# Indirect gathers of a graph convolution, issued without their bounds check

## The reference

```
deg  = segment_sum(1, dst);  norm = deg[src]**-0.5 * deg[dst]**-0.5
for (W, b) in three layers:
    h = segment_sum((h @ W)[src] * norm, dst) + b
out = layernorm(x + h)
```

## Time and profile before

| | us |
|---|---|
| three executions, median | 3550.75 (3549.87 to 3553.59) |
| span of the profiled execution | 3868.5 |
| GpSimd busy in it | 2587.0 (67%) |
| TensorE busy in it | 2756.2 (71%) |
| VectorE busy | 1462.3 (38%) |
| ScalarE busy | 383.0 (10%) |

### The profile page before, as it was taken

The page is one execution under the profiler, slowest core; times in us unless marked ns, Lnnn a source line. Parts: engine busy times, 40 slices in busy tenths (PEclk is TensorE's granted clock), DMA queues, the critical chain, the costliest instruction groups (busy, mean ns, idle before and its releaser), DMA issues.

```text
span 3868.5 us, 33824 instructions
## 1 busy us (share of the span) xinstructions
PE 2756.2 (71%) x6732; PEld 1145.6 (30%) x6782; DVE 1462.3 (38%) x3181; ACT 383.0 (10%) x581; POOL 2587.0 (67%) x2511
## 2 busy tenths in 40 slices
PE   7677777777777767677766667675666677676675
PEld 5233333333333322222222222222222222222222
DVE  6344444544444422222222222222333333333334
ACT  1122222222222200000000000000000000000000
POOL 0677676776766747776766767666676677676765
PEclk8888888988888889988899999988998988989988
DMA  8566666666666646666666666665676666666765
GB/s 299 172 186 185 176 188 181 189 180 175 184 184 179 187 128 191 191 190 183 192 187 188 194 190 197 184 192 172 193 206 196 199 201 203 193 202 196 206 195 167
DMA packets 243709, 735.25 MB, mean 190 GB/s; under 512 B 43286, under 2 KB 44946, under 8 KB 243664
## 3 DMA queue, kind: packets, MB, share of 16 engines
q0 software_dynamic: 199440, 653.68, 59.2%
q1 hardware_dynamic: 44224, 81.08, 5.8%
HBM read 683.39 MB, written 51.20 MB: 190 GB/s over the span
## 4 chain that ended last, share of the span: by engine, by line
issue 22%; another core or an unknown queue 13%; PE 9%; POOL 7%; DMA 6%; DVE 4%; DVEq 2%; POOLq 1%; SPq 0%; ACT 0%; ACTq 0%
PE ps L587 9%; POOL ring L427 7%; DMA ring<-y_dram,idx_stage 5%; DVE acc L966 1%; DVEq L963 1%; DVE onehot L923 1%; DVE idx_stage L914 1%; POOLq L427 0%; DMA y_dram<-acc 0%; DVE h_sb L988 0%; DVEq L966 0%; DVE ln L994 0%; DMA out_dram<-row_sb 0%; DVE h_sb L974 0%
## 5 line engine op out<-in xcount | busy, mean ns | idle before, releaser
L427 POOL DMA_INDIRECT ring<-y_dram,idx_stage x2493 | 2584.1, 1037 | 1258.0 <-issue 761.4
L587 PE MATMUL ps<-ring,onehot 128*128 128x512 f32 x4570 | 2293.4, 650 | 833.7 <-DMA ring<-y_dram,idx_stage 586.8
L587 PEld LDWEIGHTS ps<-ring,onehot 128*128 128x128 f32 x4570 | 910.3, 207 | 2148.4 <-issue 1800.6
L914 DVE COPY idx_stage<-src_idx 128x4 int32 (+1 forms) x624 | 111.9, 180 | 1836.4 <-remote 767.8
L966 DVE SCALAR_TENSOR_TENSOR acc<-ps,mask,acc 128x512 f32 x624 | 440.1, 745 | 91.3 <-issue 74.0
L923 DVE TENSOR_TENSOR onehot<-place_iota,lo_f 128x512 f32<-128x512 f32 (+1 forms) x624 | 400.9, 643 | 1.1 <-issue 0.6
L611 PE MATMUL ps<-w,w_sb 128*128 128x512 f32 x376 | 225.9, 757 | 127.5 <-issue 89.6
L717 ACT ACTIVATE acc<-h_sb,dinv 128x512 f32 (+1 forms) x96 | 69.3, 722 | 1399.3 <-DVE h_sb L974 901.8
L611 PEld LDWEIGHTS ps<-w,w_sb 128*128 128x128 f32 x376 | 91.0, 249 | 243.8 <-issue 199.8
L721 ACT ACTIVATE ln<-ln 128x1 f32<-128x1 f32 x49 | 9.9, 203 | 1231.2 <-DVE ln L1000 586.3
L594 PE MATMUL ps<-wT,w_sb 128*128 128x512 bf16 x234 | 82.3, 409 | 54.1 <-DVE wT L945 51.3
(11 more groups left out here) (121 smaller groups left out, 783.8 us busy)
## 6 DMA issues: line engine op xcount, KB each, us to landing
ring<-y_dram,idx_stage POOLq DMA_INDIRECT x2493
y_dram<-acc SPq DMA_DIRECT2D x96, 256.0 KB
acc<-in_x_dram SPq DMA_DIRECT2D x1, 12288.0 KB
y_dram<-acc SPq DMA_DIRECT2D x12, 1024.0 KB
w_sb<-in_x_dram SPq DMA_DIRECT2D x48, 256.0 KB
out_dram<-row_sb SPq DMA_DIRECT2D x48, 256.0 KB
w_sb<-in_L_gnn_W_dram SPq DMA_DIRECT2D x2, 1024.0 KB
w<-in_L_gnn_W_dram SPq DMA_DIRECT2D x1, 1024.0 KB
```

The lines of the kernel that those rows point to most:

```text
L427: pool.indirect_dma_start(ring[:, s, :], None, y_dram[layer], bass.IndirectOffsetOnAxis(ap=idx_stage[:, s:s + 1], axis=0), bounds_check=N ...
L587: mm = pe.matmul(ps[:, bank, :], onehot[:, r, k, :], ring[:, r * CPQ + k, :], start=(opens and k == splits), stop=(closes and k == chunks ...
L914: dve.tensor_copy(idx_stage[:, r * CPQ:(r + 1) * CPQ], src_idx[:, bass.ds(CPQ * quad, CPQ)]).then_inc(idx_staged, 1)
```

## The change

The gather is given neither a bound nor the flag for indices beyond it:

```diff
             def gather(layer, s, landed):
                 pool.indirect_dma_start(ring[:, s, :], None, y_dram[layer],
-                                        bass.IndirectOffsetOnAxis(ap=idx_stage[:, s:s + 1], axis=0),
-                                        bounds_check=N - 1, oob_is_err=False).then_inc(landed, 16)
+                                        bass.IndirectOffsetOnAxis(ap=idx_stage[:, s:s + 1], axis=0)).then_inc(landed, 16)
```

## The result

| | us |
|---|---|
| before, median of 4 | 3550.99 (3549.87 to 3553.59) |
| changed, median of 4 | 3439.18 (3427.92 to 3444.91) |
| ratio | 0.968 (0.9663 to 0.9698) |
| span of the changed kernel's profiled execution | 3443.0 |

The change saves 111.8 us, 3.2%. The direction and the range (3395 to 3560) were right. The forecast of 53 us was less than half of what came.

The account below looks back on a forecast made before the run. POOL's cadence of 1.30 us a gather was taken as the bound for some four fifths of the run. 47 us from the check plus 6 us from restarts made 53 us, so 3550.75 became 3498 us, range 3395 to 3560.

Parts of the forecast that it names:

- The bound: POOL's gather cadence of 1.30 us bounds some four fifths of the run, TensorE the rest.
- The register moves: 2493 moves of 29 ns, 72 us of POOL's queue, are hidden behind descriptor writing except where POOL has stopped.
- restarts: Where POOL resumes after waiting, 168 times, the move is exposed; removing it saves 5 to 10 us, taken as 6.
- The wait that moves: Waits for stored tables pass from the register move to the gather: cost 0, within 3 x 0.9 us.
- The check itself: Comparing indices with the bound in POOL's descriptor writing costs 25 ns a gather, between 0 and 155; 62 us in all.
- The share that arrives: Three quarters of the 62 us off POOL's chain reaches the run time, 47 us; TensorE's pace absorbs the rest.
- Rival 1: Comparison on POOL costs nothing, only the moves count: 3545 us, from 3541 to 3551; chance 0.30 together with Rival 4.
- Rival 2: The check in POOL's gather is dear, 49 to 155 ns: 3453 to 3255 us; chance 0.15.
- Rival 3: Without a bound, POOL's descriptor writing takes a path dearer by 49 ns: 3655 us, slower; chance 0.13.
- Rival 4: POOL still checks, with the table's size as bound; only moves go, time as Rival 1; chance 0.30 together with it.
- What to look for: New profile: gather median near 973 ns or cadence near 1.275 us, index waits above 340.8 us, TensorE's row waits below 741.
- A slip in the range: Concerns the forecast's own range for the check, 10 to 49 ns a gather, 3528 to 3453 us; chance 0.42.

Follow-up runs that it names:

- experiment 6: Kernel before with the check kept but its register set once, so no register moves, on the quicker chip: 3553.4 us, ratio 0.9999.
- experiment 5: Changed kernel, unaltered, run again beside the kernel before on the quicker chip: 3443.3 us against 3553.4, ratio 0.9694.
- experiment 10: Kernel before, check and moves kept, with only its onehot tiles built by four single-input instructions: 3508.6 us against 3549.6, ratio 0.9885.
- experiment 8: Changed kernel with onehot built by four single-input compare instructions in place of one with two SBUF inputs: 3385.4 us, ratio 0.9529.
- experiment 12: Changed kernel with single-input onehot instructions and three bf16-split chunks in a step of layer one instead of four: 3347.9 us against 3549.6, ratio 0.9433.
- experiment 9: Changed kernel with a 128x96 memset on POOL before every gather, its count awaited by VectorE before staging: 3559.4 us, ratio 1.0026.
- experiment 11: Kernel before with bound 3124 in place of 6249 except in the first step, so about half the rows are not gathered: 3502.0 us in one run.
- experiment 3: Kernel before with the check and moves kept but the out-of-bounds error flag true, on the slower chip: 3854.1 us, ratio 0.9948.
- experiment 4: Changed kernel, no check, with the out-of-bounds error flag false, on the slower chip: 3852.9 us, ratio 0.9946.
- experiment 1: Kernel before, no edit, profiled once more, on the slower chip: 3868.0 us, median of 11 runs 3873.5 us.

## Why the prediction was right or wrong, point by point

**The bound.** Right that POOL's cadence is the bound; wrong in how far. I gave it four fifths of the run and TensorE the rest. On the quicker chip POOL never waits for indices, with the check or without (experiments 6 and 5). The 340.8 us of waits for indices that I read out of the earlier trace rows belong to the slower chip. I saw that the profiled execution was 9% longer than the runs and reasoned that nothing hung on it; a difference larger than the effect should have made me ask which waits in it were real.

**The register moves.** Nothing is seen of them, as the cover of the earlier trace rows said: ratio 0.9999 in experiment 6, with the reserve of up to 10 us that stands there. The 6 us for restarts fail in any case: I counted 157 restarts before staged indices, of which 65 were only the usual gap between two gathers; on the quicker chip there are three, at the table stores.

**The wait that moves.** Nothing clear, as predicted, to a few us. Experiment 10 is the kernel on the quicker chip in which the move still carries the wait; POOL's three long waits for stored tables are 152.5 us in it, and 145.9 to 149.7 us in experiments 5, 6, 8 and 12, which have no move ahead of a gather. No run tests this alone.

**The check itself.** This is the step that failed, by its size. I put it at 25 ns, and it measured 52 ns (998 to 946), or 56 against experiment 6. With 52 ns in place of 25 my own sum gives 2493 x 52 ns x 0.75 + 6 = 103 us against the measured 111.8. The row nearest in kind gave 49 ns (282 - 233), and I halved it for the chance that several indices are looked at together. Unhalved it would have given 92 + 6 = 98 us. Halving between "nothing" and the nearest row gave a value that neither case would show. That the nearest row came so close may be luck; no run shows that the same instructions are behind both.

**The share that arrives.** Three quarters, for TensorE's share of the pace. Measured: 111.8 of 2493 x 52 = 130 us is 86%; between the traces of experiments 6 and 5 it is 102.3 of 140 us or 73%, and 78% in the reverse test (experiment 9). The number was near by luck and the reason wrong: POOL waits for nobody, and the rest is lost to gathers that begin under a two-input instruction. The prediction did not have these, though 1037 ns of mean against 998 of median stood in the earlier trace rows.

**Rivals.** Rival 1, only the moves count: refuted by experiment 6. Rival 2, a dear check: its lower end of 49 ns is what came, within 3 to 7 ns. Rival 3, another path without a bound: refuted by 946 and 949 ns with either flag; the flag costs 17 ns, but only with a bound. Rival 4: refuted, as the writing got shorter.

**What to look for.** The cadence in full flow was to be near 1.275 us and is 1.251. TensorE's waits for rows were to fall, and they did on one chip: 661.7 + 196.5 = 858.2 us with the check (experiment 6), 607.4 + 170.1 = 777.5 us without (experiment 5). The 741 us of the earlier trace rows were read on the slower chip and can't be held against either. POOL's waits for staged indices were to grow beyond 340.8 us; on the quicker chip there are none but the usual gap. The bytes are the same 653.68 MB.

**A slip in the range.** 10 ns a gather give 2493 x 10 ns x 0.75 + 6 = 25 us and so 3526 us as the upper end of the forecast, not 3528. Nothing hangs on it.

## What to carry to other kernels

Where one engine issues thousands of equal instructions back to back, most of the kernel's time is the mean of that one instruction, with the gap before it, times its count. Take out of it what the data does not need, then look at its records above the median and at what was already running when they began. Before a saving is sized, compare the profiled execution with the timed runs; if they differ by more than the effect, find out which waits belong to the kernel and which to that execution. An unknown between zero and a measured row is two cases, not their mean.

## What the runs showed of the hardware

- The check of 128 indices against a bound costs 52 to 56 ns of the 998 to 1002 ns of descriptor writing. With half of the bytes left out the median is still 998 ns (experiment 11, one run). The error flag adds 17 ns with a bound (experiment 3) and at most 3 ns either way without one (experiment 4).
- A skipped index keeps its packets: 199440 in both, with half the bytes.
- POOL has a gap of 0.30 us between gathers in which a memset of 0.12 us is free. With one of 0.19 us the cadence grows by 0.06.
- A gather that begins while VectorE is in an instruction with two tensors from SBUF is longer by what is left of that instruction, less some 0.12 us (up to 1.05 us in experiment 5). One that has begun before the instruction is not longer, nor is one beside an instruction with one of its two inputs in PSUM. Beside single-input instructions of 128x128 it is 0.016 us on average. Building `onehot` with these is worth 58 us here.
- Two chips ran the same program in 3550 and 3873 us. A gather (998 ns) and VectorE's add (746 ns) last as long on both, in experiments 10 and 1. On the slower one the granted clock was 0.89 to 0.90 and not 0.93 to 0.94, and VectorE staged up to 12.5 us after the quad's end in the stretch shown. Why is open, and so is how much of the check's price arrives on it.
